# A four-layer graph network on one core: the second layer's edge sums move from VectorE into PSUM

## The reference, cut to what matters

```python
d = gelu(layer_norm(gelu(layer_norm(x3 @ Wd1 + bd1)) @ Wd2 + bd2))   # per edge
w1, w2, w3 = h @ W1, h @ W2, h @ W3
logits = w1[target] - w2[source] + d
e = exp(logits - segment_max(logits)[target])
a = e / segment_sum(e)[target]
out = segment_sum(a * (w3[source] + d), target)
```

## Time and profile before

| | us |
|---|---|
| median of 3 runs | 2112.9 (2112.38 to 2113.97) |
| the profiled execution, its own time | 2112.08 |
| its span, first to last instruction | 2110.3 |
| second layer: first gather | 630.79 |
| second layer: last gather issued | 1104.25 |
| second layer: first gather of last rows (L632) | 1138.52 |

### The profile page before, as it was taken

One profiled execution on the slowest core, in us unless ns is written; L12 is line 12 of the kernel. 1 busy time (PEld: TensorE's weight loads), 2 busy tenths in 40 slices (PEclk: granted clock), 3 DMA queues, 4 the chain that ended last, 5 costly groups with the idle time before them and its releaser, 6 DMA issues. The chain is left out here.

```text
span 2110.3 us, 23002 instructions
## 1 busy us (share of the span) xinstructions
PE 1472.3 (70%) x6831; PEld 1142.4 (54%) x6831; DVE 1570.8 (74%) x2458; ACT 900.5 (43%) x1176; POOL 1348.8 (64%) x1404
## 2 busy tenths in 40 slices
PE   2777777877644666666662299999967428999990
PEld 1555655645543554555551177777745226877770
DVE  6877677767655898898995767777768367999882
ACT  1333333333226666776751144444437213434340
POOL 5777777777627777767773377777700417777754
PEclk9776676666666887787775599999975558999995
DMA  5422222222223554555552244444435313434331
GB/s 127 108 80 75 84 74 82 81 76 81 76 59 108 156 175 154 178 175 179 174 167 89 68 89 93 91 95 96 93 90 182 95 25 75 111 93 106 92 91 37
DMA packets 216424, 220.57 MB, mean 105 GB/s; under 512 B 107182, under 2 KB 170115, under 8 KB 216067
## 3 DMA queue, kind: packets, MB, share of 16 engines
q1 hardware_dynamic: 167555, 147.32, 23.6%
q0 software_dynamic: 45024, 58.36, 12.9%
q10 hardware_dynamic: 3744, 13.63, 1.7%
HBM read 117.72 MB, written 101.46 MB: 104 GB/s over the span
## 5 line engine op out<-in xcount | busy, mean ns | idle before, releaser
L605 POOL DMA_INDIRECT gathered<-table,idx x1272 | 1232.8, 969 | 528.7 <-issue 391.5
L1670 DVE COPY_PREDICATED spare<-spare,psum 64x512 f32<-64x512 uint8 x294 | 216.6, 737 | 145.8 <-ACT spare L1290 106.1
L941 PE MATMUL psum<-rounded 128*128 128x512 f32 x1092 | 266.2, 401 | 23.8 <-DVE rounded L1772 23.8
L941 PEld LDWEIGHTS psum<-rounded 128*128 128x128 f32 x1092 | 206.9, 193 | 66.7 <-issue 24.1
L638 POOL DMA_INDIRECT arena<-scan,rowidx x100 | 102.3, 1023 | 190.4 <-DMA scan<-ea 124.2
L1290 ACT ACTIVATE spare<-psum 64x512 f32<-64x512 f32 x82 | 48.3, 589 | 315.6 <-PE psum L941 315.0
L1092 ACT ACTIVATE arena<-psum 128x1024 f32<-128x1024 f32 x52 | 53.2, 1024 | 235.6 <-PE psum L728 143.7
L742 PE MATMUL psum<-ident,arena 128*128 128x128 f32 x416 | 99.5, 385 | 41.6 <-DVE arena L1522 20.8
L1772 DVE TENSOR_SCALAR_CACHE_REDUCE rounded<-spare,rowcol 128x1024 fp32r<-128x1024 uint16 x105 | 128.3, 1265 | 0.0
L941 PE MATMUL psum<-rounded_keep 128*128 128x512 f32 x480 | 127.4, 414 | 0.0
L1531 DVE TENSOR_TENSOR arena<-gathered,wgt 128x512 f32<-128x512 f32 x52 | 36.2, 696 | 116.6 <-DMA gathered<-table,idx 116.5
(11 more groups left out here) (270 smaller groups left out, 3449.7 us busy)
## 6 DMA issues: line engine op xcount, KB each, us to landing
scan<-arena SPq DMA_DIRECT2D x52, 768.0 KB, 4.0
scan<-ostage SPq DMA_DIRECT2D x130, 256.0 KB, 2.2
gathered<-table,idx POOLq DMA_INDIRECT x1272
d_mlp<-arena ACTq DMA_DIRECT2D x26, 512.0 KB, 2.7
arena<-d_mlp SPq DMA_DIRECT2D x52, 256.0 KB, 4.4
ea<-in_edge_attr SPq DMA_DIRECT2D x104, 128.0 KB
spare<-src_row SPq DMA_DIRECT2D x98, 128.0 KB, 3.4
spare<-src_quarter SPq DMA_DIRECT2D x98, 96.0 KB, 3.1
```

The source lines that it names most:

```text
L605: pool.indirect_dma_start(out=out[:, j, hf, :], out_offset=None, in_=tab[layer], in_offset=bass.IndirectOffsetOnAxis(ap=idx[:, j, hf * NCH ...
L941: last = nc.tensor.matmul(P[:, bank + t, :], parts[layer][n][:, b:b + 2, :].rearrange("p b d -> p (b d)"), tile(layer, m, u)[:, hf * CH:(h ...
L1670: picked = v.copy_predicated(rows[m % 2][halves[hf], :], quarter[m % 2][halves[hf], q - 1, :], P[halves[q % 2], bank + q // 2, :])
```

## The change: what it does

- PE adds `d` itself. `l1_logits` multiplies the identity by the `d` tile (float32, 512 columns) into a PSUM bank and then adds w2 to it: 4 matmuls of 128 columns against the identity in place of the 4 transposes, or one matmul of the picked rows. `l1_values` does the same for w3 in bank 1.
- The logits lie in bank 0 or 7 by turns. DVE's maximum scan and its second subtraction read them there; e times values reads bank 1 and now stands after the scan of the sums. The two additions (L1686, L1691) are gone, and with them the semaphores "logits made" and "u made".
- PE's values(c) now stand in step c, after the sums of c-1; they wait for the product of c-1 ("eu made"). Before, both inputs of c+1 stood together in step c.
- `d` has three buffers. A buffer is loaded again after "in transposed", thus after values(c).
- ACT's first-quarter copies stand at the head of a step, ahead of the exponential, not after the masks.

The core of the diff (what is left out renames and passes the chunk number on):

```diff
-        dch = [a(CH) for _ in range(2)]
+        dch = [a(CH) for _ in range(3)]
...
-                if c + 2 < NCH:
-                    sp.wait_ge(S("u made", c % 2), past(c // 2 + 1))
-                    load_d(c // 2 + 1, c % 2)
+                if c + 3 < NCH:
+                    sp.wait_ge(S("in transposed", c % 2), n_in_transposed(1, c // 2 + 1))
+                    load_d(c + 3)
...
+            def l1_logits(c):
+                k, bank = c % 2, 7 * (c % 2)
+                pe.wait_ge(S("d loaded", c % 3), 16 * (c // 3 + 1))
+                pe.wait_ge(S("diff made", k), past(c // 2))
+                nc.tensor.matmul(P[:, bank, :], ident[:, :], dch[c % 3], start=True, stop=True)
                 if c in FETCHED[1]:
                     g = FETCHED[1].index(c)
                     pe.wait_ge(S("L1 split", g % 2), past(g // 2 + 1))
-                    pe.wait_ge(S("logits made", 1 - k), past(i + k))
                     for j in range(J):
-                        last = nc.tensor.transpose(P[:, 0, j::J], wsplit[g % 2][:, j * 128:(j + 1) * 128], ident[:, :])
...
+                        last = nc.tensor.matmul(P[:, bank, j::J], wsplit[g % 2][:, j * 128:(j + 1) * 128], ident[:, :],
+                                                start=False, stop=True, skip_group_check=True)
...
+            def l1_values(c):
+                k = c % 2
+                pe.wait_ge(S("eu made", 1 - k), past(c // 2 + k))
+                nc.tensor.matmul(P[:, 1, :], ident[:, :], dch[c % 3], start=True, stop=True)
...
             for c in range(NCH):
                 l1_out_m(c // 2, c % 2)
                 if c + 1 < NCH:
-                    l1_in(c + 1)
+                    l1_logits(c + 1)
                 if c:
                     l1_out((c - 1) // 2, (c - 1) % 2)
+                l1_values(c)
                 l1_multiply_after(c)
...
             for c in range(NCH):
+                for hf, ahead in ((0, 5), (1, 2)):
+                    if c + ahead in MULTIPLIED[1]:
+                        l1_first_quarter(MULTIPLIED[1].index(c + ahead), hf)
                 act.wait_ge(S("diff made", c % 2), past(c // 2 + 1))
                 nc.scalar.activation(soft[c % 2], soft[c % 2], ACT.Exp).then_inc(S("expd made", c % 2), 1)
...
-                v.tensor_tensor(soft[k][:, CH:2 * CH], P[:, 0, :], dch[k], ALU.add).then_inc(S("logits made", k), 1)
-                v.tensor_tensor(val[k], P[:, 1, :], dch[k], ALU.add).then_inc(S("u made", k), 1)
-                v.tensor_tensor_scan(mrun[k][:, 1:CH + 1], neg[k], soft[k][:, CH:2 * CH], mrun[k][:, 0:1],
+                v.tensor_tensor_scan(mrun[k][:, 1:CH + 1], neg[k], logits, mrun[k][:, 0:1],
...
-                v.tensor_tensor(val[k], num, val[k], ALU.mult).then_inc(S("eu made", k), 1)
...
                 v.tensor_tensor_scan(srun[k], damp, num, srun[1 - k][:, CH - 1:CH],
                                      ALU.mult, ALU.add).then_inc(S("s scanned", k), 1)
+                dve.wait_ge(S("in transposed", k), n_in_transposed(1, i + 1))
+                v.tensor_tensor(val, num, P[:, 1, :], ALU.mult).then_inc(S("eu made", k), 1)
```

More of the change, by code:

```diff
@@ L87, in build @@
         ring_unit = {
-            "L0 msg made": 1, "L1 w2 transposed": 1, "L1 split": 1, "d loaded": 16,
+            "L0 msg made": 1, "L1 w2 transposed": 1, "L1 split": 1,
             "damp made": 1, "diff made": 1,
@@ L91, in build @@
             "evacuated": 1, "expd made": 1, "hidden made": 1, "hidden summed": 1,
-            "L2 scan stored": 16, "d stored": 16, "in transposed": 1,  "logits made": 1, "m carried": 1,
+            "L2 scan stored": 16, "d stored": 16, "in transposed": 1, "m carried": 1,
             "m evacuated": 1, "m scanned": 1, "m transposed": 1, "neg made": 1,
@@ L95, in build @@
             "s scanned": 1, "scan stored": 16, "scanned": 1,
-              "u made": 1,
         }
@@ L283, in build @@
         a = take(0)
-        dch = [a(CH) for _ in range(2)]
+        dch = [a(CH) for _ in range(3)]
         neg = [a(CH) for _ in range(2)]
         soft = [a(2 * CH) for _ in range(2)]
-        val = [a(CH) for _ in range(2)]
+        val = a(CH)
         wsplit = [a(2 * CH) for _ in range(2)]
@@ L492, in _, with load_d @@
             node_table(1, "w3 copied", tabs)
-            def load_d(i, k):
-                sp.dma_start(dch[k], d_dram[:, at(i, k)]).then_inc(S("d loaded", k), 16)
+            def load_d(c):
+                sp.dma_start(dch[c % 3], d_dram[:, at(c // 2, c % 2)]).then_inc(S("d loaded", c % 3), 16)
             for slot in range(2):
                 sp.wait_ge(S("d stored", slot), past(NQ, 16))
-            for k in range(2):
-                load_d(0, k)
+            for c in range(3):
+                load_d(c)
             sp.wait_ge(*stage("w1 copied b"))
@@ L856, in l1_out @@
                 last.then_inc(S("out transposed", k), 1)
-            def l1_in(c):
-                i, k = c // 2, c % 2
+            def l1_logits(c):
[3 more added lines that the diff above has]
+                nc.tensor.matmul(P[:, bank, :], ident[:, :], dch[c % 3], start=True, stop=True)
                 if c in FETCHED[1]:
@@ L875, in l1_in @@
                     pe.wait_ge(S("L1 quarters picked", 1), m + 1)
[L876 to L881, removed]
+                    last = nc.tensor.matmul(P[:, bank, :], W[:, W2NEG, :], rows[m % 2], start=False, stop=True,
+                                            skip_group_check=True)
+                last.then_inc(S("L1 w2 transposed", k), 1)
+            def l1_values(c):
+                k = c % 2
+                pe.wait_ge(S("eu made", 1 - k), past(c // 2 + k))
+                nc.tensor.matmul(P[:, 1, :], ident[:, :], dch[c % 3], start=True, stop=True)
+                if c in FETCHED[1]:
+                    g = FETCHED[1].index(c)
+                    for j in range(J):
+                        last = nc.tensor.matmul(P[:, 1, j::J], wsplit[g % 2][:, CH + j * 128:CH + (j + 1) * 128],
+                                                ident[:, :], start=False, stop=True, skip_group_check=True)
+                else:
+                    last = nc.tensor.matmul(P[:, 1, :], W[:, W3, :], rows[MULTIPLIED[1].index(c) % 2], start=False,
+                                            stop=True, skip_group_check=True)
+                last.then_inc(S("in transposed", k), 1)
             def l1_multiply(m, hf, blocks):
@@ L910, in _ @@
             pe.wait_ge(*stage("h1 split"))
-            l1_in(0)
+            l1_logits(0)
             for c in range(NCH):
@@ L1245, in _ @@
                     l1_negate(c + 2)
-                for hf, ahead in ((0, 5), (1, 2)):
-                    if c + ahead in MULTIPLIED[1]:
-                        l1_first_quarter(MULTIPLIED[1].index(c + ahead), hf)
                 l1_onehots_after(c)
@@ L1676, in _ @@
             split_table(1, h, "h1 split")
+            for slot in range(2):
+                dve.wait_ge(S("d stored", slot), past(NQ, 16))
             step(v.memset(mrun[1][:, CH:CH + 1], -BIG))
@@ L1682, in l1_max @@
                 i, k = c // 2, c % 2
-                dve.wait_ge(S("d loaded", k), past(i + 1, 16))
-                dve.wait_ge(S("L1 w2 transposed", k), past(i + 1))
-                dve.wait_ge(S("scanned", k), n_scanned(1, i))
-                v.tensor_tensor(soft[k][:, CH:2 * CH], P[:, 0, :], dch[k], ALU.add).then_inc(S("logits made", k), 1)
+                logits = P[:, 7 * k, :]
                 dve.wait_ge(S("m transposed", k), past(i))
```

9 lines of the change are left out of this document (4 added, 5 removed).

## The result

The changed kernel takes 2143.7 us (median of 4 runs, 2140.18 to 2145.98) against 2112.64 for the kernel before: a ratio of 1.0148, 95% interval 1.0133 to 1.0162. It is slower by 31 us where I forecast 14 less, and outside my range. The profiled execution took 2140.18, with a span of 2138.5.

A forecast was written before the change was run, and what follows sets the result against it. GpSimd's gather pace was taken to bound the second layer; 9.1 us less waiting for the split and 5.2 less contention gave -14.3, so 2098 us. Forecast 2090 to 2106, whole range 2085 to 2115.

The forecast's parts named there:

- GpSimd sets the pace of this stretch: Second layer: back-to-back gathers, 1.25 us from start to start, bound it, 10.0 us a fetched chunk against VectorE's 7.79.
- The waits for the split go: GpSimd's waits for ACT's split in the second layer disappear: 9.1 us saved, bounds 0 and 9.1.
- my reason: With ACT's first quarter ahead of the exponential, the pick runs before the gather lands; GpSimd's two buffers cover the split's delay.
- Contention falls by half: Second layer's short gather excess, 10.5 us, halves because two of four elementwise instructions keep both operands in SBUF: 5.2 us saved.
- not beside scans: Claim that the short gather excess comes beside VectorE's four elementwise instructions, with gathers beside scans taking 0.94 us.
- the short excess: 69 second-layer gathers some 0.15 us longer than normal, in pairs once per VectorE chunk, 10.5 us in all.
- my four elementwise instructions: VectorE's run L1698 to L1709, beside which the prediction placed the short gather excess; two keep both operands in SBUF.
- another kind: 11 longer gathers, the longest 1.90 us, 6.8 us in all, counted apart from the 69 short ones.
- TensorE: Second layer: its work grows to 390 to 410 us at a clock of 0.85 to 0.9, covered by GpSimd's pace.
- Rival 1: TensorE sets the second layer's pace at a clock under 0.72: 17 us slower, 2129 us, chance 0.17.
- Where VectorE's freed time went: VectorE needs 0.9 us a chunk less, 47 over the layer; hidden by GpSimd's pace, it buys only slack.
- End of the layer: From the second layer's last split to its last scan: 22.4 to 25.1 us against 23.8 before, taken as no difference.

The follow-up runs named there:

- The kernel with the damping in PSUM: Changed kernel, but the damping factor is written to PSUM bank 7, so both sum and output scans have one SBUF input; logits use bank 0 alone: 2096.9 us.
- the kernel before with the product between: Kernel before the change, with VectorE's product e times values moved between the sum and output scans, nothing else: 2163.2 us, ratio 1.0237.
- the changed kernel with the quarters back: Changed kernel with ScalarE's first-quarter copies moved back behind the masks: 2146.7 us, ratio 1.0155 to the kernel before.
- the kernel before with the quarters first: Kernel before the change, with only ScalarE's first-quarter copies moved to the head of a step: 2104.7 us, ratio 0.996.
- The swap alone: Product e times values moved ahead of the sum scan in the changed kernel: 2113.5 us; moved behind it in the kernel before: 2163.2 us.
- the table: Ten kernels: the one before, the changed one, and eight single-edit variants of either, from 2096.9 to 2163.2 us.
- the kernel before with the damping in PSUM: Kernel before the change, with the damping factor written to PSUM bank 7 and both additions kept: 2110.9 us, ratio 0.9988.

## Why the prediction was wrong

- *GpSimd sets the pace of this stretch*: right, and the account of its phase (intervals, waits, queue gaps, excess) holds to the end. The kernel with the damping in PSUM has the phase at 451.9: 438.4 of plain intervals, 5.4 of excess, 6.5 of queue gaps and 1.6 of waits.
- *The waits for the split go*: they went, all of them, as did VectorE's for the quarters: -9.1, as summed. But the result is no proof of my reason. With gathers this slow the waits go in any case: they are also gone in the kernel before with the product between (ScalarE's order as it was) and in the changed kernel with the quarters back. What bears the reason out is the kernel before with the quarters first, where 0.3 us is left, and the damping in PSUM, where 1.6 is.
- *Contention falls by half, -5.2, bounds 0 and 10.5*: this is the step that failed, by sign. The excess rose by 39 us. My reading was "not beside scans": I had seen gathers of 0.94 next to scans and took it that scans with two SBUF inputs don't hold gathers. They do: a gather that starts behind one ends 0.75 after it. Even the short excess I had put in the wrong place. Of each pair the first gather is held by the maximum scan, the second by L1699; of my four elementwise instructions the other three hold almost none. What I had seen was a sample that the two engines' lockstep had chosen: 0 gathers in the harmful 0.8 us behind 52 sum scans, 1 behind 52 output scans. With GpSimd's 1.25 us from gather to gather, chance would have put some 33 there (an estimate: 52 x 0.8 / 1.25). The maximum scan could have told me: all 40 gathers behind it were held, 9 of them long, out of the 11 that I had filed under another kind. The Trainium skill's rule was cited in the prediction, and I set it aside on that sample.
- *Nothing that the change does moves the scans* was never said, and had to be asked: I priced the new place of the product at the 0.10 of its semaphore and did not look at the distance between the scans, 1.38 then and 1.9 now. The swap alone is worth 30 us in the changed kernel and 50 in the one before.
- *TensorE*: 0.91 of the clock (forecast 0.85 to 0.9), 398 us busy from 647 to 1160 (390 to 410), and hidden. Rival 1 was wrong though it had the sign: GpSimd waits for nothing in the phase that TensorE could be behind, and the swap of two VectorE instructions takes 30 of the 31 us away.
- *Where VectorE's freed time went*: into waiting for TensorE's logits, which is waiting for gathers, 152.8 us in the layer. It paid for nothing.
- *End of the layer*: 1.8 us shorter than before, where I took no difference, and 0.4 under my lower bound.

With the damping in PSUM the kernel took 2096.9, faster than both kernels and next to my 2098. That is luck. Its excess is 12.0 us lower than before, more than the 5.2 of my sum and than its bound of 10.5, its phase is 21.6 us shorter and not 14, and its profiled execution took 2090.77; the six runs go from there to 2102.1.

## What to carry to other kernels

Where VectorE and GpSimd's indirect DMAs both run all the time, count for each VectorE instruction how many inputs it takes from SBUF, and list by where each gather starts relative to it how long it takes and how far behind the instruction's end it ends. A fixed distance of the two ends gives a hold away even when it is short. An offset that never occurs in the trace is not an offset that costs nothing: two engines in step hide it, and any reordering brings it out. Moving one input of a long two-input instruction to PSUM took it out of the game here, and the scan stayed at 1.28 us.

## What the runs showed of the hardware

- A scan of 128 x 512 float32 with two SBUF inputs held every gather that started 0.11 to 1.05 us behind the scan's start, in every kernel of the table that has such scans; the gather ended 0.75 to 0.76 us after the scan's end (1.94 long at most). A gather that started ahead of the scan or with it was not held by it: 43 that started with the old sum scan, to 0.01 us, took 0.94 or 0.95. VectorE lost nothing measurable in return: scans last 1.28 either way.
- With either input in PSUM, 1.28 as well, and no gather is held (48, 36, 31 and 18 of them in two kernels).
- An elementwise instruction with two SBUF inputs (0.69) does the same for its shorter life: the gather ends 0.81 to 0.82 after it, and is up to 1.46 long behind L1705.
- After gathers 113, 225 and 337, thus every 112, the queue pauses for 2.0 to 5.9 us in the kernels of the table. One pause is shorter, 0.6, and follows a wait of 2.9 for the split (the kernel before with the damping in PSUM).
